# Moving the last 64-row block of a relational basis mix from TensorE to ScalarE and GpSimd, with interleaved one-hots

## The chip, the cores and the metric

One core of one Trainium2 chip. The time is that of one execution of the whole program on the device, in microseconds; less is better. Before the change, three runs took 917.99, 918.70 and 922.83 us, median 918.7 us.

## The reference

A graph of 1250 nodes (512 features) and 21250 edges goes through four graph layers, each followed by a residual sum and a layer norm:

```python
x = _layernorm(x + _L0_gnn_ref(x, edge_index, ...))    # GCN, batch norm, gelu
x = _layernorm(x + _L1_gnn_ref(x, src, dst, ...))      # two SAGE layers
x = _layernorm(x + _L2_gnn_ref(x, edge_index, edge_type_2, ...))   # two relational layers
x = _layernorm(x + _L3_gnn_ref(x, edge_index, ...))    # GIN
```

A relational layer first mixes its weights out of 30 bases of 512 x 512 f32 numbers, for two relations: `w = einsum('rb,bio->rio', att, basis)`. The change is about this mix for the first of the two relational layers.

## The kernel before

The kernel opens with a count stage. It turns the edge list into a dense matrix of edge counts, source node by target node and relation, which all later layers use as a matmul operand. The target nodes are cut into 40 windows of 32 nodes. The edges are sorted by target, in 170 chunks of 128 edges, and a window covers five or more chunks. For each chunk VectorE makes two f16 one-hot matrices in SBUF: `oh_lo` (128 edges x 128, the low 7 bits of the source; stationary operand) and `oh_key` (128 x 640, made of target in the window, relation and source tile; moving operand). TensorE multiplies them (L572, two matmuls of 320 columns a chunk) and sums over the window's chunks in PSUM.

- VectorE, `windows` (L1155): for each window `lows_of` (L1151) makes the four fixed chunks' `oh_lo` in one tensor_tensor (is_equal of an iota and of `lo_h`, whose innermost step is 0); `key_of` (L1140) makes one `oh_key` each; a loop makes `oh_lo` and `oh_key` (L1145, L1140) of the chunks beyond four (one in most windows, two in some). It waits until TensorE has finished the window before the last (`s_win`), so it can be about one window ahead. Once in four windows `sum_counts` (L1178, L1180) adds the two relations of a finished tile. Between windows 9 and 14 it also reduces the input's maximum (L1285, L1288) and a weight's (L1216), and after window 17 computes scales.
- ScalarE, `tile_out`: copies each window's PSUM to SBUF (L766), copies turned tiles out (L772), copies a finished group of the mix (L779) and stores it by DMA (L782), and from window 19 on splits one input tile every second window (L807, L809).
- GpSimd: subtracts to make the low half of each of these ten input tiles (L547, f32 and f16 operands in SBUF).
- TensorE, after each window's product: turns a tile's counts (L597), degrees (L605), and then `mix` (L620): the first relational mix. The stationary operand `mixT` holds attention factors times a folded identity, the moving one a pair of bases' 64 rows (128 partitions x 512 f32). 15 matmuls, one a pair of bases, sum up 64 rows of both relations (partitions 0 to 63 and 64 to 127) in PSUM bank `T[:, 1]`. There are 8 such groups. Group 0 runs ahead of window 0; the other 105 matmuls are handed out by `GROUP_BLOCKS`, two or three after each window.
- SyncE issues the loads in a fixed order: `load_mix` into 8 slots, each when TensorE has freed the slot (`s_mx`).

After window 39 the first unit's dense matmuls begin (L666), for which ScalarE issues DMA transposes (L828) and TensorE turns the last counts (L597). The semaphore `s_mxst` guards the mix results in DRAM (`mixd`), which the fourth unit reads.

Of the kernel before, what the change touches and what calls it, by code (L numbers as in the profile page):

```python
# [8 lines left out]
P = 128  # L9
# [9 lines left out]
FIXED = 2  # L19
# [7 lines left out]
GROUPS = 2 * KT  # L27
MIX_SLOTS = 8
# [20 lines left out]
def resnorm_gnn_kernel(nc, x, src_t, dst_t, typ_t, dst_r, W0, b0, gamma, beta,  # L49
# [11 lines left out]
    with ctx:  # L61
# [86 lines left out]
        dstr = hview(4 * 2 * P).bitcast(i32).rearrange("p (g e) -> p g e", g=2)  # L148
        wlo = hview(4 * NWIN).bitcast(f32)
# [14 lines left out]
        mix_in = [stage[:, q, :] for q in range(KT)] + [zview(4 * D).bitcast(f32) for _ in range(MIX_SLOTS - KT)]  # L164

# [50 lines left out]
        s_xin, s_xmax, s_s0 = sem("s_xin"), sem("s_xmax"), sem("s_s0")  # L216
# [3 lines left out]
        s_gmax = sem("s_gmax")  # L220
# [4 lines left out]
        s_eye, s_mixT = sem("s_eye"), sem("s_mixT")  # L225
        mx_full = [sem(f"mx_full{i}") for i in range(MIX_SLOTS)]
        s_mx = sem("s_mx")
        s_mxe = sem("s_mxe")
        s_mxst = [sem(f"s_mxst{i}") for i in range(2)]
# [36 lines left out]
        b_idf, b_one, b_dg, b_row, b_rev = (sem("b_" + n) for n in ("idf", "one", "dg", "row", "rev"))  # L266
# [24 lines left out]
        GROUP_BLOCKS = [6, 6, 6, 6, 5, 5, 6]  # L291
        assert sum(GROUP_BLOCKS) == NWIN and len(GROUP_BLOCKS) == GROUPS - 1
# [139 lines left out]
        Z_SCALED = 38  # L432
# [17 lines left out]
        def _(sp):  # L450
# [50 lines left out]
        def _(pool):  # L501
# [13 lines left out]
            pool.partition_all_reduce(rngr, rng, P, RMAX).then_inc(s_rngr, 1)  # L515
            pool.memset(epsc[:, :], EPS).then_inc(s_const, 1)
            pool.memset(onec[:, :], 1.0).then_inc(s_const, 1)
            pool.memset(ones, 1.0).then_inc(b_one, 1)
# [22 lines left out]

            pool.wait_ge(s_xin, 1)
            pool.partition_all_reduce(xmax[:, :], xin[:, :], P, RMAX).then_inc(s_xmax, 1)
# [12 lines left out]
            pool.partition_all_reduce(gmax[:, :], gin[:, :], P, RMAX).then_inc(s_gmax, 1)  # L556
# [10 lines left out]
        def _(pe):  # L567

            def chunk_product(slot, j, start=False, stop=False):

                for b in range(2):
                    last = nc.tensor.matmul(Dp[:, j, b, 0:HALF], oh_lo[:, ds(slot * P, P)],  # L572
# [52 lines left out]
            pe.wait_ge(s_const, 10)  # L625
# [11 lines left out]
            assert mixed[0] == PAIRS * GROUPS  # L637
            pe.wait_ge(s_ate, 5 * (NT - 1))
            pe.wait_ge(s_mxe, GROUPS)
# [118 lines left out]
        def _(act):  # L758
# [804 lines left out]
```

## Time and profile before

| | |
|---|---|
| median of three runs | 918.7 us |
| the profiled execution | 917.2 us |
| its span, first to last instruction | 915.4 us |
| TensorE matmul busy | 882.8 us, 96% |
| VectorE busy | 656.2 us, 72% |
| ScalarE busy | 280.8 us, 31% |
| GpSimd busy | 87.9 us, 10% |

The shares are means over the whole program, whose stages have different limits; the count stage is its first 183.66 us.

### The profile page before, as it was taken

Reading aid. Unit: us, or ns where it says so; the run is one execution under the profiler, and the core shown is the slowest. Engines: PE = TensorE matmul, PEld = TensorE weight load, DVE = VectorE, ACT = ScalarE, POOL = GpSimd, SP = SyncE. Lnnn points to the kernel's source line nnn. Section 1 sums busy time; section 2 is a strip of 40 time slices with the busy share of each in tenths; the row PEclk is TensorE's granted clock in tenths of the full one; section 3 lists DMA queues with packets and bytes.
Section 4 is the critical chain, followed back from the end, with each engine's and each line's share of the span. In section 5 each row is a group of like instructions: output and inputs, shape, how many; then the busy total and the mean of one; then the engine's idle time right before and its main releaser. Section 6 shows DMA issues by size and latency. Waiting matters only on the chain.

```text
span 915.4 us, 12673 instructions
## 1 busy us (share of the span) xinstructions
PE 882.8 (96%) x4258; PEld 428.2 (47%) x4258; DVE 656.2 (72%) x1286; ACT 280.8 (31%) x431; POOL 87.9 (10%) x66
## 2 busy tenths in 40 slices
PE   7999999999959999899997999999999999999997
PEld 3555555554545444344443444444444444444443
DVE  6898978658987797998999988975324255552247
ACT  0333444637752116222312111114311221132221
POOL 1000111301220003021210000003200020020000
PEclk9999999999979999999998999999999999999999
DMA  8955665596435885788464655530131014322228
GB/s 275 352 168 165 183 188 191 149 238 198 155 95 157 200 236 150 208 207 204 128 150 108 155 141 161 139 91 1 35 81 23 12 47 139 82 62 41 47 60 237
DMA packets 134888, 129.50 MB, mean 141 GB/s; under 512 B 80687, under 2 KB 81156, under 8 KB 134826
## 3 DMA queue, kind: packets, MB, share of 16 engines
q10 hardware_dynamic: 96192, 60.25, 26.1%
q1 hardware_dynamic: 38634, 68.45, 24.9%
q8 instruction: 36, 0.59, 0.3%
q14 instruction: 26, 0.21, 0.1%
HBM read 97.80 MB, written 12.52 MB: 121 GB/s over the span
## 4 chain that ended last, share of the span: by engine, by line
PE 68%; DVE 15%; DMA 8%; ACT 4%; issue 2%; POOL 1%; DVEq 1%; ACTq 0%; SPq 0%
PE Dp L696 25%; PE Dp L666 24%; PE T L620 11%; PE Dp L572 6%; DVE acc L1262 4%; DMA stage<-in_basis 3%; DMA wst<-mixd 2%; DMA xr<-xres 2%; DVE Zraw L1373 1%; ACT W L1010 1%; DVE stt L1354 1%; ACT wst L863 1%; DVE w L1391 1%; PE T L666 1%; POOL Zraw L530 1%
## 5 line engine op out<-in xcount | busy, mean ns | idle before, releaser
L666 PE MATMUL Dp<-W,hT 128*128 128x512 f16 x792 | 175.7, 381 | 3.6 <-DMA hT<-S 3.6
L696 PE MATMUL Dp<-Zraw,A 128*128 128x512 f16 x800 | 173.0, 379 | 0.0
L1262 DVE SCALAR_TENSOR_TENSOR acc<-stage,att,acc 128x512 f32<-128x512 f32 x232 | 163.5, 770 | 4.3 <-DMA stage<-in_basis 4.3
L696 PE MATMUL Dp<-Zraw,AT 128*128 128x512 f16 x600 | 130.0, 379 | 0.0
L666 PEld LDWEIGHTS Dp<-W,hT 128*128 128x128 f16 x792 | 77.8, 98 | 96.6 <-DMA hT<-S 3.8
L696 PEld LDWEIGHTS Dp<-Zraw,A 128*128 128x128 f16 x800 | 78.2, 98 | 94.4
L696 PEld LDWEIGHTS Dp<-Zraw,AT 128*128 128x128 f16 x600 | 58.7, 98 | 70.8
L1140 DVE TENSOR_SCALAR Zraw<-hT,w 128x640 f16<-128x640 f16 (+1 forms) x209 | 85.9, 456 | 0.3
L1391 DVE SCALAR_TENSOR_TENSOR w<-Dp,aggc,S 128x512 f32<-128x512 f32 x40 | 29.9, 747 | 59.9 <-PE Dp L696 54.0
L962 ACT ACTIVATE Zraw<-Dp,zsc 128x512 f16<-128x512 f32 x46 | 29.4, 684 | 125.8 <-PE Dp L666 121.7
L620 PE MATMUL T<-stage,W 128*128 128x512 f32 x120 | 60.5, 627 | 5.5 <-DMA stage<-in_basis 5.5
L572 PE MATMUL Dp<-Zraw 128*128 128x320 f16 (+1 forms) x418 | 63.7, 299 | 0.4 <-DVE Zraw L1140 0.3
L1331 DVE SCALAR_TENSOR_TENSOR Zraw<-Dp,zsc,Zraw 128x512 f16<-128x512 f32 x26 | 19.5, 749 | 58.6 <-ACT Zraw L962 58.6
L1001 ACT ACTIVATE w<-w,s_in 128x512 f32<-128x512 f32 x30 | 21.6, 720 | 121.0 <-DVE w L1391 116.0
L530 POOL TENSOR_TENSOR W<-wst,W 128x1024 f16<-128x1024 f32 x18 | 42.8, 2395 | 158.6 <-ACT W L866 158.6
L572 PEld LDWEIGHTS Dp<-Zraw 128*128 128x128 f16 (+1 forms) x418 | 40.6, 98 | 36.9 <-issue 23.2
L620 PE MATMUL T<-Zraw,W 128*128 128x512 f32 x120 | 57.4, 601 | 0.0
L666 PE MATMUL Dp<-W,stage 128*128 128x512 f16 x240 | 52.8, 379 | 1.2 <-DVE Zraw L1331 1.2
L766 ACT ACTIVATE Zraw<-Dp 128x640 f16<-128x640 f32 x40 | 28.1, 703 | 78.4 <-PE Dp L572 76.3
L721 PE MATMUL Dp<-AT,Zraw 128*128 128x512 f16 (+1 forms) x240 | 43.4, 344 | 0.0
L1151 DVE TENSOR_TENSOR Zraw<-hT,Zraw 128x512 f16<-128x512 f16 x40 | 28.5, 712 | 20.8 <-PE Dp L572 15.0
L962 ACT ACTIVATE Zraw<-Dp 128x512 f16<-128x512 f32 x26 | 15.5, 596 | 74.6 <-PE Dp L666 72.0
(176 smaller groups left out, 950.4 us busy)
## 6 DMA issues: line engine op xcount, KB each, us to landing
stage<-in_basis SPq DMA_DIRECT2D x180, 256.0 KB, 2.9
Zraw<-in_basis SPq DMA_DIRECT2D x60, 256.0 KB, 3.1
xres<-w ACTq DMA_DIRECT2D x30, 256.0 KB, 2.3
xr<-xres ACTq DMA_DIRECT2D x30, 256.0 KB, 3.1
wst<-in_Wn ACTq DMA_DIRECT2D x4, 1024.0 KB, 5.6
wst<-in_Ws ACTq DMA_DIRECT2D x4, 1024.0 KB, 6.0
wst<-mixd ACTq DMA_DIRECT2D x4, 1024.0 KB, 6.0
wst<-in_root ACTq DMA_DIRECT2D x3, 1024.0 KB, 6.7
```

The lines of the kernel that those rows point to most:

```text
L530: pool.tensor_tensor(weights_of(u, m)[:, 1, 2 * h:2 * h + 2, :], source, weights_of(u, m)[:, 0, 2 * h:2 * h + 2, :], ALU.subtract).then_in ...
L572: last = nc.tensor.matmul(Dp[:, j, b, 0:HALF], oh_lo[:, ds(slot * P, P)], oh_key[:, ds(slot * KEYS + b * HALF, HALF)], start=start, stop=stop)
L620: nc.tensor.matmul(T[:, 1, :], mixT[:, b * P:(b + 1) * P], mix_in[n % MIX_SLOTS], start=(b == 0), stop=(b == PAIRS - 1)).then_inc(s_mx, 1)
L666: last = nc.tensor.matmul(dense_bank(u, t, m), turned[:, hp, k * P:(k + 1) * P], weights_of(u, m)[:, wp, k, :], start=(n == 0), stop=(n == ...
L696: last = nc.tensor.matmul(sum_bank(t), a[:, k, ds(t * P, P)], Z[:, r, h, k, :], start=(n == 0), stop=(n == count - 1))
L721: last = nc.tensor.matmul(Df[:, j, c:c + w], Z[:, 0, h, k, b * P:(b + 1) * P], AT[:, k, c:c + w], start=(k == 0 and h == 0), stop=(k == NT ...
L766: nc.scalar.activation(B[:, t % 2, :, :, a:a + WIN].rearrange("p s r (b d) -> p b (s r) d", b=2), Dp[:, w % 2, 0:2, 0:HALF].rearrange("p b ...
L962: nc.scalar.activation(Z[:, r, 0, ds(t, 1), :], dense_rows(u, t, r), ACT.Copy, scale=scale).then_inc(s_zhi[u], 1)
L1140: return v.tensor_scalar(oh_key[:, ds(slot * KEYS, KEYS)], iota_n, wkey[:, w:w + 1], key_f[:, ds(c, 1)], ALU.add, ALU.is_equal)
L1151: v.tensor_tensor(oh_lo[:, slot * P:(slot + n) * P].rearrange("p (c k) -> p c k", c=n), iota_n[:, 0:P].rearrange("p (c k) -> p c k", c=1). ...
L1262: last = v.scalar_tensor_tensor(part, stage[:, q, :], a, part, ALU.mult, ALU.add)
L1391: v.scalar_tensor_tensor(w1[:, j:j + 1, :], sum_bank(t).rearrange("p (a d) -> p a d", a=1), c, rest, ALU.mult, ALU.add).then_inc(s_pre[u], 1)
```

## The change

- The mix on TensorE has 7 groups instead of 8: 105 matmuls in all instead of 120, 90 of them handed out after windows (`GROUP_BLOCKS` from `[6, 6, 6, 6, 5, 5, 6]` to `[7, 7, 7, 7, 6, 6]`).
- The last 64 rows of both relations are made elsewhere. Per basis, two DMAs of 64 rows each bring the same 64 rows of one basis into partitions 0 to 63 and 64 to 127 of a `bias` buffer (two buffers). After windows 8 to 37 ScalarE scales one basis by its attention column (`late_scaled`), in place, and GpSimd adds it to `late_sum` (29 adds; the first basis is scaled straight into the sum). After window 39 ScalarE stores the sum by two DMAs (`late_out`).
- SyncE's loads are interleaved: `load_late(b)`, which waits until the buffer's add is done (`l_done`), then the next two or three `load_mix`.
- `lows_of` writes the four fixed chunks' `oh_lo` interleaved (chunk innermost), and TensorE reads each as stationary operand with a step of four elements. A new iota, each number repeated four times, stands against `lo_h`, so that no operand has an innermost step of 0.
- Some semaphores are merged, and one initial wait counts the new iota.

```diff
+PE_GROUPS = GROUPS - 1
+LATE_FROM = 8
-        GROUP_BLOCKS = [6, 6, 6, 6, 5, 5, 6]
+        GROUP_BLOCKS = [7, 7, 7, 7, 6, 6]
...
+            for r in range(REL):
+                sp.dma_start(late_att[r * 64:(r + 1) * 64, :], att1[2 + r:3 + r, :].broadcast_to([64, BASES])).then_inc(e_att, 16)
+            def load_late(b):
+                wait(sp, l_done, b - 1)
+                for r in range(REL):
+                    sp.dma_start(late_in[b % 2][r * 64:(r + 1) * 64, :],
+                                 basis1[PE_GROUPS, b // 2, b % 2 * 64:(b % 2 + 1) * 64, :]).then_inc(l_full[b % 2], 16)
+            at = PAIRS + 2 * NT
+            for b in range(BASES):
+                nxt = PAIRS + 2 * NT + (PAIRS * PE_GROUPS - PAIRS - 2 * NT) * (b + 1) // BASES
+                load_late(b)
+                load_mix(at, nxt)
+                at = nxt
+            sp.wait_ge(l_done, BASES)
...
+            def late_add(end):
+                for b in range(late[0], end):
+                    pool.wait_ge(l_sc, b + 1)
+                    if b:
+                        pool.wait_ge(l_done, b)
+                        pool.tensor_tensor(late_sum, late_sum, late_in[b % 2], ALU.add).then_inc(l_done, 1)
+                    else:
+                        pool.sem_inc(l_done, 1)
+                late[0] = end
+            late_add(6)
             pool.wait_ge(s_xin, 1)
...
+            late_add(8)
             reduce_weights(0)
             for t in range(NT):
+                late_add(12 + 2 * t)
                 pool.wait_ge(x_hi, t + 1)
...
+                if isinstance(slot, int):
+                    n = 2 * FIXED
+                    four = slot // n * n
+                    low = oh_lo[:, four * P:(four + n) * P].rearrange("p (k c) -> p k c", c=n)[:, :, slot % n]
+                else:
+                    low = oh_lo[:, ds(slot * P, P)]
...
+            def late_out():
+                act.wait_ge(l_done, BASES)
+                for r in range(REL):
+                    act.dma_start(mixd[r, PE_GROUPS * 64:GROUPS * 64, :],
+                                  late_sum[r * 64:(r + 1) * 64, :]).then_inc(s_mxst[PE_GROUPS % 2], 16)
+            def late_scaled(b):
+                if b == 0:
+                    act.wait_ge(e_att, 64)
+                act.wait_ge(l_full[b % 2], 16 * REL * (b // 2 + 1))
+                nc.scalar.activation(late_in[b % 2] if b else late_sum, late_in[b % 2], ACT.Copy,
+                                     scale=late_att[:, b:b + 1]).then_inc(l_sc, 1)
             def tile_out(t):
                 for i in range(PER):
                     w = PER * t + i
                     window_out(w)
+                    if 0 <= w - LATE_FROM < BASES:
+                        late_scaled(w - LATE_FROM)
...
             for t in range(NT):
                 tile_out(t)
                 weight_work("counts", 0, t)
-            act.wait_ge(s_const, 10)
+            late_out()
+            act.wait_ge(s_const, 11)
...
-                v.tensor_tensor(oh_lo[:, slot * P:(slot + n) * P].rearrange("p (c k) -> p c k", c=n),
-                                iota_n[:, 0:P].rearrange("p (c k) -> p c k", c=1).broadcast_to([P, n, P]),
-                                lo_h[:, ds(c, n)].rearrange("p (c k) -> p c k", k=1).broadcast_to([P, n, P]), ALU.is_equal)
+                v.tensor_tensor(oh_lo[:, slot * P:(slot + n) * P].rearrange("p (k c) -> p k c", c=n),
+                                iota_c.rearrange("p (k c) -> p k c", c=n),
+                                lo_h[:, ds(c, n)].rearrange("p (k c) -> p k c", k=1).broadcast_to([P, P, n]), ALU.is_equal)
```

## Rows read from the trace of the kernel before

**Rows 1.** Busy time by stretch: bounds, length, busy time (count) per engine, clock, DMA.
```profile
21.20:58.75 37.55, 37.55 (x195) 20.99 (x193) 29.95 (x80) 12.14 (x20) 0.00 (x0) 1.00 0.84 285
58.75:133.35 74.60, 74.23 (x425) 41.92 (x424) 65.24 (x165) 31.40 (x53) 6.30 (x7) 1.00 0.59 178
133.35:183.66 50.31, 50.31 (x283) 28.41 (x280) 36.13 (x85) 27.01 (x43) 13.20 (x8) 1.00 0.59 172
```
**Rows 2.** The chain that ended last: start, length, what.
```profile
46.91 1.36 PE Dp L572 x10
...
93.49 1.82 PE T L620 x4
...
129.14 1.36 PE Dp L572 x10
130.50 0.22 PE Dp L597 x4
130.72 2.63 PE T L620 x6
...
183.66 0.91 issue
```
**Rows 3.** Waits of VectorE, 53.8 to 125 us: total, times, longest.
```profile
DVE Zraw L1151 <- PE Dp L572: 0.6, 1, 0.6
```
**Rows 4.** The same, 125 to 176 us.
```profile
DVE Zraw L1151 <- PE Dp L572: 8.9, 6, 2.1
```
**Rows 5.** VectorE and TensorE in order of time: start, length, instruction, idle before it.
```profile
48.49 0.69 DVE L1151 TENSOR_TENSOR Zraw<-hT,Zraw 128x512 f16<-128x512 f16 x1 [1.00 <-PE Dp L572]
...
53.86 0.69 DVE L1151 TENSOR_TENSOR Zraw<-hT,Zraw 128x512 f16<-128x512 f16 x1 [0.62 <-issue]
...
75.02 1.15 DVE L1140 TENSOR_SCALAR Zraw<-hT,w 128x640 f16 x3
...
75.09 1.95 PE L572 MATMUL Dp<-Zraw 128*128 128x320 f16 x10 [0.27 <-DVE Zraw L1140]
...
123.78 1.15 DVE L1140 TENSOR_SCALAR Zraw<-hT,w 128x640 f16 x3
...
174.43 1.33 DVE L1140 TENSOR_SCALAR Zraw<-hT,w 128x640 f16 x3
```
**Rows 6.** Groups by line and shape, 0 to 240 us: busy, mean ns.
```profile
L1151 DVE TENSOR_TENSOR Zraw<-hT,Zraw 128x512 f16<-128x512 f16 x40 | 28.5, 712 | 20.8 <-PE Dp L572 15.0 <-issue 5.7
...
L1178 DVE TENSOR_TENSOR AT<-Zraw 128x1280 f16<-128x1280 f16 x10 | 8.2, 816 | 5.8 <-ACT Zraw L766 5.8
```
**Rows 7.** VectorE's small tensor_tensor and two key pairs, in order of time.
```profile
103.25 0.23 DVE L1180 TENSOR_TENSOR AT<-AT,ident 128x128 f16<-128x128 f16 x1
...
104.70 0.80 DVE L1140 TENSOR_SCALAR Zraw<-hT,w 128x640 f16<-128x640 f16 x2
...
107.31 1.64 DVE L1140 TENSOR_SCALAR Zraw<-hT,w 128x640 f16<-128x640 f16 x2
...
152.02 1.06 DVE L1180 TENSOR_TENSOR AT<-AT,ident 128x128 f16<-128x128 f16 x1
```
**Rows 8.** GpSimd in order of time (three of ten such subtractions).
```profile
107.59 1.16 POOL L547 TENSOR_TENSOR S<-w,S 128x512 f16<-128x512 f32 x1 [6.88 <-ACT S L809]
...
124.63 1.31 POOL L547 TENSOR_TENSOR S<-w,S 128x512 f16<-128x512 f32 x1 [4.74 <-ACT S L809]
...
150.97 2.02 POOL L547 TENSOR_TENSOR S<-w,S 128x512 f16<-128x512 f32 x1 [7.23 <-ACT S L809]
```
**Rows 9.** Weight loads by line and shape, 0 to 240 us: busy, mean ns.
```profile
L572 PEld LDWEIGHTS Dp<-Zraw 128*128 128x128 f16 x320 | 31.0, 98 | 32.9 <-issue 22.8 <-DVE Zraw L1140 0.7 <-ACT Zraw L766 0.5
...
L620 PEld LDWEIGHTS T<-stage,W 128*128 128x128 f32 x120 | 22.1, 199 | 25.3 <-issue 19.3 <-DVE W L1093 5.4 <-DMA stage<-in_basis 0.5
```
**Rows 10.** ScalarE's scaling of a tile, its wait for TensorE, SyncE's wait.
```profile
L807 ACT ACTIVATE w<-acc,s_in 128x512 f32<-128x512 f32 x8 | 5.8, 727 | 2.4 <-issue 2.4
...
ACT Zraw L766 <- PE Dp L572: 75.2, 35, 3.6
...
SPq L458 <- PE T L620: 110.7, 92, 3.3
```
**Rows 11.** Behind the count stage, in order of time.
```profile
184.50 1.13 ACTq L782 DMA_DIRECT2D mixd<-gw  x2
...
191.46 0.23 DVE L1315 CAST gw<-ident 128x128 f32<-128x128 f16 x1
...
192.74 0.61 ACT L772 ACTIVATE A<-Dp 128x512 f16<-128x512 f32 x1
193.04 0.65 PEld L597 LDWEIGHTS Dp<-ident,Zraw 128*128 128x128 f16 x8
```

More of the change, by code:

```diff
@@ L148, in resnorm_gnn_kernel @@
         dstr = hview(4 * 2 * P).bitcast(i32).rearrange("p (g e) -> p g e", g=2)
+        iota_c = dstr.bitcast(f16).rearrange("p g e -> p (g e)")
         wlo = hview(4 * NWIN).bitcast(f32)
@@ L164, in resnorm_gnn_kernel @@
         mix_in = [stage[:, q, :] for q in range(KT)] + [zview(4 * D).bitcast(f32) for _ in range(MIX_SLOTS - KT)]
+        late_att = att[:, 0, :]
+        late_in = [bias[:, i, :] for i in range(2)]
+        late_sum = zview(4 * D).bitcast(f32)
         W2 = W[:, 2, :, :, :].rearrange("p h k d -> p (h k d)")
@@ L228, in resnorm_gnn_kernel @@
         s_mxe = sem("s_mxe")
+        l_full = [sem(f"l_full{i}") for i in range(2)]
+        l_done = sem("l_done")
+        l_sc = sem("l_sc")
         s_mxst = [sem(f"s_mxst{i}") for i in range(2)]
@@ L265, in resnorm_gnn_kernel @@
         s_xst = {u: [sem(f"s_xst{u}_{j}") for j in range(2)] for u in LN}
-        b_idf, b_one, b_dg, b_row, b_rev = (sem("b_" + n) for n in ("idf", "one", "dg", "row", "rev"))
+        b_dg, b_row, b_rev = (sem("b_" + n) for n in ( "dg", "row", "rev"))
         b_ev, b_st, b_mv, b_sd, b_co, b_g = (sem("b_" + n) for n in ("ev", "st", "mv", "sd", "co", "g"))
@@ L289, in resnorm_gnn_kernel @@
         DG = Dp[:, 1, 2, 0:2 * NT]
-        GROUP_BLOCKS = [6, 6, 6, 6, 5, 5, 6]
-        assert sum(GROUP_BLOCKS) == NWIN and len(GROUP_BLOCKS) == GROUPS - 1
+        GROUP_BLOCKS = [7, 7, 7, 7, 6, 6]
+        assert sum(GROUP_BLOCKS) == NWIN and len(GROUP_BLOCKS) == PE_GROUPS - 1
         SHARES = [(i + 1) * PAIRS // n - i * PAIRS // n for n in GROUP_BLOCKS for i in range(n)]
@@ L431, in resnorm_gnn_kernel @@
         XS_FROM = 19
-        Z_SCALED = 38
+        Z_SCALED = 39
         def halves_split(u):
@@ L515, in _ @@
             pool.partition_all_reduce(rngr, rng, P, RMAX).then_inc(s_rngr, 1)
+            pool.iota(iota_c, [[1, P], [0, 2 * FIXED]], base=0, channel_multiplier=0, **kw).then_inc(s_const, 1)
             pool.memset(epsc[:, :], EPS).then_inc(s_const, 1)
             pool.memset(onec[:, :], 1.0).then_inc(s_const, 1)
-            pool.memset(ones, 1.0).then_inc(b_one, 1)
+            pool.memset(ones, 1.0).then_inc(s_const, 1)
             def reduce_weights(u):
@@ L569, in chunk_product @@
             def chunk_product(slot, j, start=False, stop=False):
+                if isinstance(slot, int):
[4 more added lines that the diff above has]
+                    low = oh_lo[:, ds(slot * P, P)]
                 for b in range(2):
-                    last = nc.tensor.matmul(Dp[:, j, b, 0:HALF], oh_lo[:, ds(slot * P, P)],
+                    last = nc.tensor.matmul(Dp[:, j, b, 0:HALF], low,
                                             oh_key[:, ds(slot * KEYS + b * HALF, HALF)], start=start, stop=stop)
@@ L624, in _ @@
             mix(PAIRS)
-            pe.wait_ge(s_const, 10)
+            pe.wait_ge(s_const, 11)
             pe.wait_ge(s_tbl, 1)
@@ L869, in load_bias @@
             def load_bias(u):
+                if u == 1:
+                    act.wait_ge(l_done, BASES)
                 if u > 2:
@@ L1087, in _ @@
             dve.wait_ge(s_const, 8)
-            v.tensor_tensor(eye, ident[:, 0:P // 2], ident[:, P // 2:P], ALU.add).then_inc(s_eye, 1)
-            dve.wait_ge(s_eye, 1)
+            link(v.tensor_tensor(eye, ident[:, 0:P // 2], ident[:, P // 2:P], ALU.add))
             def mix_table(a0, a1):
@@ L1135, in _ @@
             dve.wait_ge(s_tbl, 1)
-            dve.wait_ge(s_const, 8)
+            dve.wait_ge(s_const, 9)
             def key_of(w, slot, c):
```

28 lines of the change are left out of this document (13 added, 15 removed).

## The prediction

> **What bounds the kernel now.** I read the busy time by stretch, the chain of waits, VectorE's waits, and then VectorE and GpSimd in order of time. In the count stage TensorE is busy in all but 0.4 of 162 us [rows 1], and the chain consists of its products (L572) and mix matmuls (L620) with hardly a gap [rows 2]. So TensorE bounds the stage, but VectorE stands close behind. From the one-hots of window 10 (53.86) to the last key of window 27 (123.78 + 1.15 = 124.93) it waited for TensorE 0.6 us in 71.07 [rows 3, 5]. Only from there to 175.76 (174.43 + 1.33) does it have room, 8.9 us in 50.8 [rows 4, 5]. In window 14 TensorE was even held by it: ten products took 1.95 us instead of the 1.36 of the chain [rows 2, 5].
>
> **TensorE's part.** Four L620 records, two matmuls, last 1.82 us in the chain, and six 2.63 [rows 2]; the difference is 0.81 to 0.88 a matmul. I take 0.87. Fifteen fewer are 13.1 us off TensorE. By GROUP_BLOCKS they leave as follows: through window 9, 25 become 21 (3.5 us); windows 10 to 27, 47 become 39 (7.0); windows 28 to 39, 33 become 30 (2.6). What is left of this depends on VectorE.
>
> **VectorE's part, gain.** The 40 four-chunk one-hots take 0.71 us each, a tensor_tensor of 512 elements. The one of 1280 elements whose innermost step is 1 throughout takes 0.82 [rows 6], and that of 128 takes 0.23 [rows 7]. On the line between them 512 elements take 0.43. Undisturbed the old form takes 0.69 [rows 5], so I take 0.26 saved per window, 10 us in all. Bounds: nothing (its rows of four elements may hold it at the old rate) to 0.35; a loss I exclude, since the new form has as many elements and no operand that is read worse than one at a time. The Trainium skill (VectorE: DVE Perf Modes, What auto-detection actually checks) says that 16-bit tensors with step 1 go at two a cycle; by the two measured durations the trace agrees, and by that rule alone the gain would be the same.
>
> **VectorE's part, cost.** This is the step on which I decide. GpSimd's subtraction of 512 elements (1.16 us) began at 107.59, within VectorE's pair of keys, which then took 1.64 us instead of 0.80 [rows 7, 8]. At 150.97 GpSimd's took 2.02, and the small tensor_tensor of VectorE behind it 1.06 instead of 0.23 [rows 7, 8]. The two engines hold each other up: of ten subtractions in the stage seven lengthened VectorE's instruction by 0.83 to 0.89, one by 0.46, and two fell largely into its idle time, as that of 124.63, after which VectorE had nothing to do anyway [rows 8]. The 29 added adds are of the same size and kind, two SBUF inputs. I price one at 0.78 us of VectorE where it is busy. Bounds: 0 (all in gaps or beside reductions) to 1.2. The Trainium skill (SBUF — State Buffer, Who interferes with whom) states a rule that speaks against this change: a two-input instruction of VectorE, or one in a two-port mode, and a GpSimd instruction share a port pair, and the loser is blocked for the whole instruction; reductions are spared. The trace agrees, with 0.84 us. By the rule's full length each add would cost 1.16, and 18 adds 7 us more than I take.
>
> **The sum, stretch by stretch.**
> Up to window 9: VectorE's window 9 waits for the products of window 7 (46.91 + 1.36 = 48.27, start 48.49 [rows 2, 5]). Two mix matmuls are gone ahead of it, 1.74, and one faster one-hot behind it, 0.26. So window 10 starts on VectorE at 53.86 − 2.0 = 51.86.
> Windows 10 to 27: VectorE's work was 71.07 − 0.6 = 70.5. Minus 18 × 0.26 = 4.7, plus 18 adds: two of them fall beside the maximum reductions, so 16 × 0.78 = 12.5. It comes to 78.3, and VectorE ends window 27 at 130.2. TensorE alone would take 7.0 less than 74.6 [rows 1], 67.6, so it is bound by VectorE there. TensorE ended window 14 0.9 us after VectorE's last key (75.09 + 1.95 = 77.04 against 75.02 + 1.15 = 76.17 [rows 5]); so window 27 ends at 131.1, against 130.5 before [rows 2]: +0.6.
> Windows 28 to 39: VectorE had 50.83 − 8.9 = 41.9. Minus 12 × 0.26 = 3.1, plus ten adds, 7.8: 46.6. TensorE needs 183.66 − 130.50 − 2.6 = 50.6 [rows 2]. TensorE bounds: the stage ends at 181.7, 2.0 us earlier than before. (VectorE would end at 176.8, and 0.9 + 0.2 + 2.6 behind it is 180.5.)
>
> **Behind the stage.** late_out puts two more DMA issues into ScalarE's queue, by the two of the row 1.13 us [rows 11]. Behind them stand the table load, the transposes, the first scaled tile and the copies of the last counts. TensorE's last turn (193.04) began right after the copy of 192.74 had its predecessor done, with some 0.2 us to spare [rows 11]; I take +0.7, bounds 0 to 1.1. VectorE's wait for the stores ahead of L1315 (191.46) is covered: they go out by about 186.8.
>
> **At nothing.** 30 scalings of 0.73 on ScalarE: it waited 75.2 us in the stage for TensorE's windows, 35 times [rows 10]; they cost 22, and a copy of a window is needed only a window later. Cover gone, a window would slip by 0.7. GpSimd is idle most of the stage, 19.5 us busy in 162 [rows 1]. SyncE: load_late(b) waits for the add of b − 2, behind which stand mix loads; at that time mixes for 1.3 windows, some 5 us, are loaded, and the queue waited for TensorE 110.7 us [rows 10]. The doubled reads of the last rows (7.9 MB for 3.9) meet DMA engines 0.59 busy [rows 1]. The fifth iota and the merged semaphores lie under the start's loads. The stationary operand with step 4: now a weight load shows 98 ns beside products of 136 (1.36 / 10), the f32 one 199 [rows 2, 9]. I take 0 (hidden up to 136); at 199 it would be 320 × 0.063 = 20 us on TensorE.
>
> Sum: −2.0 + 0.7 = −1.3 us, on 917.2 of the profiled execution (span 915.4 and 1.8 around it): 915.9. The median shown is 1.5 higher, so 917.4.
>
> **Rivals.** 0.5% of this kernel, 4.6 us, is what a measurement can tell from no change.
> (a) The adds cost VectorE little: they start mostly beside reductions, small instructions and gaps, 0 to 0.4 each. For: two of ten did. Against: VectorE has no gaps in windows 10 to 27. At 0.4, that stretch falls by 16 × 0.38 = 6.1, and the whole by 7.4: 911.3. At 0, TensorE's 13.1 less 0.7: 906.3. From 0.57 an add downward it is faster by over 4.6. Chance 0.27.
> (b) The one-hots don't gain (rows of four). Then 4.7 more in windows 10 to 27, and in the last stretch VectorE needs 49.7, still under 50.6: −1.3 + 4.9 = +3.6, 922.3. Chance 0.10, mostly under the bound.
> (c) Slower: the step of four elements lengthens the weight load. Its place is the 320 products of the fixed chunks, its price what it has beyond 136 ns, and it decides against the change from 136 + 13.1 / 320 = 177 ns. At 199 TensorE is at −13.1 + 20.2 + 0.7 = +7.8, with VectorE hidden: 926.5. Against: the f16 load has 38 ns of room. Chance 0.10.
> (d) An add costs VectorE GpSimd's whole 1.16: in windows 10 to 27 16 × 0.38 = 6.1 more, in the last stretch VectorE reaches 50.4 and ties with TensorE: +4.8, 923.5. Chance 0.08. (This is what the page on SBUF named above would make of it.)
> (e) The change doesn't bring the relief it says, because ScalarE holds a window back for a late tile (l_full): 30 waits at 0.3 would be 9 us on ScalarE, hidden by its 75. 0.02; 918.
>
> **Chances.** Forecast 0.43, own range 914.5 to 920.5. Faster: (a)'s 0.25 and 0.03 of the forecast, 0.28. Slower: (c) 0.10, (d) 0.06, (b) and the forecast's edge 0.05, 0.21. Same 0.51. The range takes in half prices of (a) and the full 1.16 of (d): 907.5 to 924.
>
> **What the profile will show.** L620 with 15 fewer matmuls; VectorE's L1151 at 0.4 us undisturbed; GpSimd with 29 adds of 1.2 us or more, each beside a VectorE instruction lengthened by 0.8; VectorE without waits for TensorE in windows 10 to 27, and TensorE instead waiting for L1140 or L1151 by some 7 us there; L572 weight loads at or near 98 ns, products at 136; first dense product at about 182.6 instead of 184.57. Wrong if TensorE keeps its gapless chain (then (a)), or if the products' pace grows (then (c)).

## The result, and the profile after

The changed kernel takes 935.4 us (median of 4 runs, 931.27 to 938.23) against 919.2 for the kernel before (917.99 to 922.83); the ratio is 1.0186, 95% interval 1.0162 to 1.0209. The forecast was 917.4 us, no change that can be measured, with a range up to 924. The kernel is slower by some 17 us, over twice the 7.8 us of the slowest rival. Below, a difference of 1% stands for 9.2 us.

| | before | after |
|---|---|---|
| span of the profiled execution | 915.4 | 929.5 |
| count stage ends, on TensorE | 183.66 | 197.30 |
| from there to the end | 731.7 | 732.2 |
| TensorE busy from 21.20 to the stage's end | 162.1 of 162.5 | 158.7 of 176.1 |

All of it lies in the count stage. The busy times by stretch, for the changed kernel, with the columns of [rows 1]:

```profile
21.20:58.75 37.55, 36.53 (x195) 21.52 (x196) 31.94 (x91) 12.92 (x22) 1.27 (x1) 1.00 0.84 283
58.75:133.35 74.60, 63.34 (x351) 36.74 (x348) 61.91 (x139) 34.61 (x58) 27.37 (x20) 0.93 0.63 181
133.35:197.30 63.95, 58.85 (x325) 33.87 (x324) 59.03 (x111) 40.70 (x66) 31.27 (x22) 0.97 0.64 191
```

TensorE, busy in all but 0.4 us before, is idle 11 us in the second stretch and 5 in the third; its granted clock is 0.93 and 0.97 there, where it was 1.00. Finer rows show where: 0.87 from 85 to 98 us, in which TensorE is busy 7.3 of 13 us, and 0.76 in the 14 us behind them. VectorE is idle too in the second (61.9 of 74.6), so it does not simply bound. GpSimd's row has 27.4 us busy of 74.6, which still looks like an engine with time to spare. Read in order of time it is not (start, length, instruction, idle before it):

```profile
9.41 0.59 POOL L541 PARTITION_ALL_REDUCE w<-w  x1 [6.43 <-issue]
17.81 1.19 POOL L542 IOTA hT<- 128x512 f16 x1 [7.81 <-issue]
...
71.11 1.26 POOL L578 TENSOR_TENSOR Zraw<-Zraw,bias 128x512 f32<-128x512 f32 x1 [2.04 <-ACT bias L847]
78.32 0.51 POOL L585 PARTITION_ALL_REDUCE xmax<-xin  x1 [5.95 <-issue]
85.84 2.67 POOL L578 TENSOR_TENSOR Zraw<-Zraw,bias 128x512 f32<-128x512 f32 x2 [7.01 <-issue]
95.56 0.38 POOL L549 PARTITION_ALL_REDUCE mwg<-mw  x1 [7.05 <-issue]
102.59 2.79 POOL L578 TENSOR_TENSOR Zraw<-Zraw,bias 128x512 f32<-128x512 f32 x2 [6.65 <-issue]
```

Each time GpSimd goes here from an iota or an add to a partition_all_reduce, or back, 5.95 to 7.81 us pass with no instruction and no one that it waits for ("issue"). The kernel before had such gaps as well, at the start and far behind the stage. Its one change inside the windows, from the reduction of 72.02 to the subtraction of 99.55, had 26.68 us of waiting for ScalarE to hide in. Its order of time shows these two, which I had not weighed:

```profile
9.77 0.65 POOL L515 PARTITION_ALL_REDUCE w<-w  x1 [6.79 <-issue]
...
266.85 0.37 POOL L556 PARTITION_ALL_REDUCE gmax<-gin  x1 [5.94 <-issue]
```

The chain of the changed kernel goes through the third gap of the stage, and its end shows who ends the stage now (start, length, what):

```profile
88.74 6.82 issue
95.56 0.39 POOL mwg L549
...
188.58 2.04 DVE Zraw L1214
190.62 2.23 DVE Zraw L1209
...
197.30 0.91 issue
```

Where TensorE's mix matmuls stood [rows 2] stand a reduction that comes late and VectorE's one-hots (L1209, L1214), far over their own 0.44 us and 0.25 us. From 96 to 193 us the chain holds 1.2 us of TensorE; nearly all the rest is VectorE and its queue. What VectorE meets at the end is not only the late adds. Behind its last instruction of the stage GpSimd makes the low half of a weight (`low_weights`, two subtractions of 1024 columns, some 2.1 us each). In the kernel before they began behind VectorE's last key (174.43 + 1.33 = 175.76); in the changed kernel they began at 188.36, inside VectorE's last window, and one low (2.12 us instead of 0.25) and the keys behind it (3.02 instead of 1.15) took 3.7 us longer. GpSimd before, GpSimd after, VectorE after:

```profile
176.91 4.21 POOL L530 TENSOR_TENSOR W<-wst,W 128x1024 f16<-128x1024 f32 x2
...
188.36 4.30 POOL L557 TENSOR_TENSOR W<-wst,W 128x1024 f16<-128x1024 f32 x2
...
188.50 2.12 DVE L1214 TENSOR_SCALAR Zraw<-hT,w 128x128 f16 x1
190.54 3.02 DVE L1209 TENSOR_SCALAR Zraw<-hT,w 128x640 f16 x3
```

The waits of the changed kernel from 40 to 200 us (total, times, longest) name the same two, and a third:

```profile
ACT bias L847 <- DMA bias<-in_basis: 23.5, 13, 4.8
DVE tmpc L1265 <- POOL mwg L549: 9.4, 1, 9.4
PE Dp L622 <- DVE Zraw L1209: 9.4, 5, 4.7
```

VectorE stood 9.4 us for the weight maximum; up to window 17 it had lost 0.4 us (its one-hots start at 83.43, at 83.02 before), and window 18 starts at 98.76 instead of 89.23. ScalarE, which also copies the windows out, waited 23.5 us for late half-tiles.

### The profile page after: what moved, and what is told of

Read it like the earlier page. It is cut to its first block, busy times and chain, and to the rows that moved or that the text cites. A ratio compares the mean times of both kernels' runs of the same rounds, so it can differ in the third digit from the quotient of the medians.

```text
span 929.5 us, 12756 instructions
## 1 busy us (share of the span) xinstructions
PE 877.6 (94%) x4228; PEld 427.6 (46%) x4228; DVE 673.1 (72%) x1286; ACT 299.0 (32%) x460; POOL 129.4 (14%) x96
## 4 chain that ended last, share of the span: by engine, by line
PE 52%; DVE 20%; issue 5%; DMA 5%; ACT 4%; DVEq 3%; POOL 1%; ACTq 0%; POOLq 0%
PE Dp L716 25%; PE Dp L746 24%; DVE acc L1331 4%; DVE Zraw L1209 3%; DVE stt L1422 1%; DVE Zraw L1441 1%; ACT W L1080 1%; DMA wst<-mixd 1%; DVE w L1459 1%; DMA stage<-in_basis 1%; ACT wst L930 1%; PE T L716 1%; DMA xr<-xres 1%; POOL Zraw L557 1%; DVEq L1233 1%
## 5 line engine op out<-in xcount | busy, mean ns | idle before, releaser
L1209 DVE TENSOR_SCALAR Zraw<-hT,w 128x640 f16<-128x640 f16 (+1 forms) x209 | 100.7, 527 | 0.5 <-issue 0.4
L622 PE MATMUL Dp<-Zraw 128*128 128x320 f16 (+1 forms) x418 | 67.1, 304 | 11.3 <-DVE Zraw L1209 10.7
L622 PEld LDWEIGHTS Dp<-Zraw 128*128 128x128 f16 (+1 forms) x418 | 45.1, 111 | 48.4 <-issue 34.4
L670 PE MATMUL T<-stage,W 128*128 128x512 f32 x106 | 56.1, 653 | 5.4 <-DMA stage<-in_basis 5.4
L578 POOL TENSOR_TENSOR Zraw<-Zraw,bias 128x512 f32<-128x512 f32 x29 | 40.5, 1397 | 89.6 <-ACT bias L847 75.6
L670 PE MATMUL T<-Zraw,W 128*128 128x512 f32 x104 | 52.4, 622 | 0.1
L549 POOL PARTITION_ALL_REDUCE mwg<-mw x7 | 2.6, 378 | 348.0 <-DVE mw L1275 340.9
```

Source lines behind the costliest of these rows:

```text
L578: pool.tensor_tensor(late_sum, late_sum, late_in[b % 2], ALU.add).then_inc(l_done, 1)
L622: last = nc.tensor.matmul(Dp[:, j, b, 0:HALF], low, oh_key[:, ds(slot * KEYS + b * HALF, HALF)], start=start, stop=stop)
L670: nc.tensor.matmul(T[:, 1, :], mixT[:, b * P:(b + 1) * P], mix_in[n % MIX_SLOTS], start=(b == 0), stop=(b == PAIRS - 1)).then_inc(s_mx, 1)
L1209: return v.tensor_scalar(oh_key[:, ds(slot * KEYS, KEYS)], iota_n, wkey[:, w:w + 1], key_f[:, ds(c, 1)], ALU.add, ALU.is_equal)
```

## The experiments

Theory at the start: GpSimd's gaps between reductions and other operations (G), on top of the forecast's port cost. Rivals: the adds alone, at a higher price than 0.78 us (A); the new one-hots or their weight loads (O); the ring of load, scale and add that holds ScalarE (R). The kernels of this section are compared with the kernel before on the same chip.

### 1 to 4: the gaps and the adds

1, the weight maximum moved next to that of x:

```diff
-            late_add(8)
             reduce_weights(0)
+            late_add(8)
```

> The two partition reductions on GpSimd in the middle of the count stage (of the input's and of a weight's maximum) stand directly behind one another, instead of with adds 6 and 7 between them. Theory S (GpSimd pays some 6 to 7 us each time it goes from tensor_tensor to the reduction or back: gaps of 5.95, 7.01, 7.05 and 6.65 us in the changed kernel's trace): two gaps of four go, VectorE's wait of 9.4 us for the weight's maximum goes, and the stage ends 5 to 8 us earlier: 928 to 931 us against 935.4. Theory P (the adds hold VectorE up at the port and nothing else matters): the same adds, no change, 935. Theory L (the late tile's ring of load, scale, add with two buffers holds ScalarE): little change, 934 to 936, since add 6 comes no earlier.

Measured: 928.7 us, ratio 1.0137 (1.0102 to 1.0172). One of the two pairs of gaps is gone, and 0.5% with it (the two intervals overlap at the edge).

2, both reductions inside the stage as plain copies, all adds kept:

```diff
-            pool.partition_all_reduce(xmax[:, :], xin[:, :], P, RMAX).then_inc(s_most, 1)
+            pool.tensor_copy(xmax[:, :], xin[:, :]).then_inc(s_most, 1)
...
-            reduce_weights(0)
+            pool.tensor_copy(mwg[:, 0:1], mw[:, 0:1]).then_inc(s_mwr, 1)
```

> Both reductions in the middle of the count stage are replaced by a copy of each partition's own maximum, so the scales are no longer those of the whole tensor (the output is not the reference's). All adds stay. Theory S: no gap of 6 to 7 us is left in GpSimd's row between 60 and 110 us; the 8.7 us lost between windows 17 and 18 come back and one or two more: 924 to 927 us. Theory P: unchanged, 935. Theory L: unchanged or 1 us less.

Measured: 926.1 us, 1.0093 (1.0071 to 1.0115). In its order of time on GpSimd the copy stands right behind an add, with no gap:

```profile
71.38 1.27 POOL L578 TENSOR_TENSOR Zraw<-Zraw,bias 128x512 f32<-128x512 f32 x1 [2.03 <-ACT bias L848]
72.58 0.79 POOL L585 COPY xmax<-xin 128x1 f32<-128x1 f32 x1
```

So the gap belongs to the change of operation and costs this kernel about half of its loss (1.0186 to 1.0093). The adds alone are not the whole cause; A falls as the only one.

3, iota_c in a buffer of its own, filled ahead of the first reduction:

```diff
+            pool.iota(iota_c, [[1, P], [0, 2 * FIXED]], base=0, channel_multiplier=0, **kw).then_inc(s_const, 1)
             pool.wait_ge(s_rng, 1)
             pool.partition_all_reduce(rngr, rng, P, RMAX).then_inc(s_rngr, 1)
-            pool.iota(iota_c, [[1, P], [0, 2 * FIXED]], base=0, channel_multiplier=0, **kw).then_inc(s_const, 1)
```

> The repeated iota has a buffer of its own and is made ahead of the first partition reduction on GpSimd, not behind it. Theory S: the gap of 7.81 us in front of it goes, VectorE makes the first one-hots at about 15.2 us as in the kernel before and not at 20.2, window 10 begins on VectorE some 2 us earlier; the later stalls stay: 932 to 934 us. Rival (the lead of 5 us is eaten by windows 10 to 14, where VectorE bounds, or by the wait for the reductions): 935, no change.

Measured: 935.4 us, 1.0216 (1.0189 to 1.0244), no gain: a miss. VectorE's first one-hots do start at 15.26 again, and window 10's at 52.17, where the forecast had 51.86. But the number of changes stays the same: the one that lay between reduction and iota lies now between reduction and the first add. That add begins 3.6 us after its half-tile is scaled (54.06 + 0.71 = 54.77 on ScalarE), where the changed kernel's begins 0.1 us after. GpSimd in order of time, in this run:

```profile
10.39 0.63 POOL L542 PARTITION_ALL_REDUCE w<-w  x1 [6.25 <-issue]
...
58.33 3.32 POOL L578 TENSOR_TENSOR Zraw<-Zraw,bias 128x512 f32<-128x512 f32 x2 [47.09 <-issue]
79.61 0.44 POOL L585 PARTITION_ALL_REDUCE xmax<-xin  x1 [7.48 <-issue]
```

The two reductions come 1.3 us later than in the changed kernel, and VectorE waits 11.0 us for the second instead of 9.4. What was won at the start was lost there.

4, no add at all (the semaphore is counted up in its place):

> GpSimd's 29 adds are left out (it only hands the semaphore on; one term of the mix remains, so the output is not the reference's). Loads, scalings and stores stay. Both S and P: TensorE bounds the stage again, 15 mix matmuls less: 908 to 912 us, some 2 us of it lost at the start through the late iota. Theory L (the loads and the scalings cost by themselves): 918 or more.

Measured: 911.9 us, 0.9942 (0.9924 to 0.996). The forecast's sum for adds at no price was 906.3 us, 0.9865. So something besides gaps and adds is missing too (this kernel keeps the start's gap ahead of the iota).

### 5 to 8: the one-hots

5, the kernel before with nothing but the interleaved one-hots (iota ahead of the reduction):

> The kernel before with only the interleaved one-hots (repeated iota in a buffer of its own, ahead of the first reduction). My forecast's step: the one-hots take 0.43 us, VectorE's windows follow each other 0.26 us sooner, TensorE still bounds: within 1 us of before, with VectorE waiting some 8 us more for TensorE. Theory Q (found in the trace of the run without adds: windows on VectorE start 2.60 us apart with one-hots of 0.43 or 0.69 alike, since its sequencer's register work sets the pace): same time, and back-to-back windows still 2.60 us apart. If the weight load with a step of four costs TensorE (rival c of the prediction), the products' pace of 136 ns grows and the time with it.

Measured: 916.9 us, 0.9984 (0.9975 to 0.9994), the only kernel that computes everything and is faster than the one before, by 1.5 us. Its groups by line and shape, 0 to 250 us (busy, mean ns, idle before):

```profile
L580 PE MATMUL Dp<-Zraw 128*128 128x320 f16 x320 | 56.5, 299 | 0.0
L580 PEld LDWEIGHTS Dp<-Zraw 128*128 128x128 f16 x320 | 36.2, 113 | 28.4 <-issue 21.7 <-ACT Zraw L774 0.5 <-DVE Zraw L1148 0.3
L1159 DVE TENSOR_TENSOR Zraw<-iota_cT,Zraw 128x512 f16<-128x512 f16 x40 | 20.1, 502 | 24.6 <-PE Dp L580 18.0 <-issue 6.3
```

The weight load with step four is 113 ns instead of 98 [rows 9] and hidden; the products stay at 299 ns, as before. That settles rival (c) of the prediction. The one-hots take 502 ns instead of 712 [rows 6], 8.4 us less in all. Of these 1.5 us come out; VectorE waits for TensorE 18.0 us instead of 15.0, and from 14 to 184 us it stands 13.1 us instead of 9.6 for nothing that the profile names ("issue").

6, 7 and 8 are the changed kernel, number 4 and number 2 with the one-hots as they were and no fifth iota:

> The changed kernel with the old form of the one-hots (and without the repeated iota and its switch on GpSimd). Forecast's step (0.26 us a window gained on VectorE): undoing it costs 4 to 7 us, less 1 to 2 for the start: 938 to 940. Theory Q: it costs nothing and the start gives 0 to 2: 933 to 935.

> As the run without adds (one term of the mix remains), and with the old one-hots. Forecast's step: 2 to 4 us slower than that run's 0.994 of before. Theory Q: the same or 1 to 2 us faster, 0.992 to 0.994 of before.

> The changed kernel with the old one-hots and both middle reductions as copies of each partition's own maximum (output not the reference's): the only long gap of GpSimd left is that in front of the first reduction. Forecast's price of the adds (0.78 us of VectorE each) with no gain from the one-hots gave 922.3 for before at 918.7, that is 1.004 of before. Theory Q together with a dearer chain of adds: 1.006 to 1.010, as the run with copies alone (1.009).

Measured: 939.5 us, 1.0251 (1.0214 to 1.0287); 910.9, 0.9928 (0.9911 to 0.9944); 929.6, 1.012 (1.0103 to 1.0137). Without adds the new one-hots bring nothing (0.9942 against 0.9928, within the intervals). With all adds and gaps they bring 0.65% (1.0251 to 1.0186), with adds and copies 0.3% (1.012 to 1.0093, intervals that overlap): they help where VectorE is held up. Why not otherwise shows in VectorE's order of time, the kernel before first and the changed one below it, windows 16 and 17:

```profile
80.42 0.69 DVE L1151 TENSOR_TENSOR Zraw<-hT,Zraw 128x512 f16<-128x512 f16 x1 [0.20 <-issue]
...
83.02 0.69 DVE L1151 TENSOR_TENSOR Zraw<-hT,Zraw 128x512 f16<-128x512 f16 x1
```

```profile
80.83 0.56 DVE L1220 TENSOR_TENSOR Zraw<-hT,Zraw 128x512 f16<-128x512 f16 x1 [0.21 <-issue]
...
83.43 0.56 DVE L1220 TENSOR_TENSOR Zraw<-hT,Zraw 128x512 f16<-128x512 f16 x1
```

Two windows follow each other by 2.60 us both times, though nothing is waited for and the one-hots are 0.13 shorter. In the chain of the changed kernel VectorE's queue (DVEq: L449, L1233, L1214) has pieces of its own between the instructions of a window. Where a late add has held VectorE up just before, the queue is ahead, and the distance does shrink: 2.28 us from 106.42 to 108.70 in the changed kernel, with one-hots of 0.41. So O has no loss in it; the gain is covered in undisturbed windows and comes out in disturbed ones.

### 9 to 12: what is left without the gaps

9, iota ahead and the two copies. One change of operation is left in the stage, between the first reduction and the first add; the prediction counted none.

> The changed kernel with the fifth iota ahead of GpSimd's first reduction (a buffer of its own) and with the two reductions inside the stage (the largest entry of x, the first weight maximum) replaced by plain copies: a scale comes out different, no value is the reference's. GpSimd then changes nowhere between a reduction and adds on the stage's path, which is what the prediction assumed. If the prediction's other terms are right (adds 0.78 us each, one-hots 0.26 us saved, TensorE 13.1 us relieved), this is its 917 us, ratio 0.996 to 1.003. If the one-hots' saving and part of TensorE's relief are not there either (windows on VectorE stay 2.60 us apart, as in the runs so far), it stays near the copies alone, 1.004 to 1.009.

Measured: 923.9 us, 1.0069 (1.0044 to 1.0094). Against the changed kernel the gaps cost 1.17%, 10.7 us. The change that is left makes the first add begin 3.9 us after its half-tile is scaled (57.93 against 53.34 + 0.71), and ScalarE waits 1.8 us for the fourth half-tile; number 13 has the same, and the changed kernel has not. It is not the forecast's 917: some 7 us have another cause.

10, number 8 with a third buffer for the late half-tiles:

> The copies in place of the two reductions, the old one-hots and no fifth iota (as in the eighth run, ratio 1.012), and a third buffer for the late half-tiles; the reductions' values are missing. If the ring of two buffers (load, scale, add, next load) held ScalarE and with it the windows, this run is 3 us or more faster than the eighth, 1.009 or less. If the adds cost by holding VectorE off, the third buffer changes nothing: 1.010 to 1.014, and VectorE's busy time per one-hot stays.

Measured: 930.5 us, 1.0127 (1.008 to 1.0173), the same as number 8. ScalarE's wait for late loads is 5.6 us, against 4.2 in number 8. The interval reaches down to 1.008, so a small gain isn't excluded, but R falls as the main cause for this spacing. It isn't nothing: the chain of number 9, with two buffers, goes once through a late half-tile, 3.43 us at 131.16.

11, number 1 and number 3 together, nothing left out:

> The changed kernel, nothing left out, with the fifth iota ahead of the first reduction and the reduction of the first weight maximum moved next to that of x's maximum. If the start's gap and the middle's gaps are separate costs, this is paired alone (1.0137) less up to 4 us, 1.009 or so. If VectorE is caught up by TensorE either way (as with the iota alone), it is 1.011 to 1.015.

Measured: 925.9 us, 1.009 (1.006 to 1.0119), as expected, though number 3 alone had gained nothing; the intervals of numbers 1 and 11 overlap. It is the best kernel with the adds in it that computes everything, and still slower than the one before.

12, the late work moved behind window 18, three items in two windows, iota ahead:

> The changed kernel, nothing left out: iota ahead, and the late half-tiles scaled and added three in two windows from window 19 on, behind both of the stage's reductions; GpSimd then changes once from reductions to adds in the stage, with nobody waiting for it, and no add falls into windows 0 to 18. TensorE's mixing shares before window 19 are as in the kernel before, its relief lies behind. If the cost is place (the gaps, and adds where VectorE bounds), window 18 is reached as before (89 us on VectorE) and the rest pays 29 adds x 0.95 = 27 us on VectorE against its idle 15 us and 13 us of relief on TensorE: a ratio of 0.997 to 1.005. If an add costs the stage the same wherever it lies (14 us for 29), it is 1.008 to 1.015.

Measured: 942.7 us, 1.0246 (1.0197 to 1.0295), a miss of both expectations. Its order of time on GpSimd, ScalarE and TensorE shows the cause (three views of one stretch, put together by time):

```profile
96.75 0.71 ACT L847 ACTIVATE bias<-bias,att 128x512 f32<-128x512 f32 x1
...
104.03 1.26 POOL L579 TENSOR_TENSOR Zraw<-Zraw,bias 128x512 f32<-128x512 f32 x1 [32.63 <-issue]
...
109.16 0.72 ACT L847 ACTIVATE bias<-bias,att 128x512 f32<-128x512 f32 x1 [6.22 <-DMA bias<-in_basis]
...
113.11 0.61 PE L647 MATMUL Dp<-ident,Zraw 128*128 128x128 f16 x4 [7.33 <-ACT A L822]
```

The scaled half-tile is there at 97.46; the add begins 6.6 us later, since the change comes in front of it (GpSimd's last operation was the reduction of 70.55). The next load needs the buffer that this add frees, ScalarE waits 6.22 us for the load, and TensorE 7.33 for a copy that stands behind it in ScalarE's queue. I had said "with nobody waiting for it". The same gap again, in a third place.

### 13 to 16: the parts of the remaining 7 us

13 is number 9 with adds of 8 columns:

```diff
-  pool.tensor_tensor(late_sum, late_sum, late_in[b % 2], ALU.add).then_inc(l_done, 1)
+  pool.tensor_tensor(late_sum[:, 0:8], late_sum[:, 0:8], late_in[b % 2][:, 0:8], ALU.add).then_inc(l_done, 1)
```

> As the ninth run (iota ahead, copies for the two reductions, 1.0069), but each of the 29 adds covers 8 columns in place of 512; every wait and GpSimd instruction is kept, most of the late sum is missing. If an add costs by the time that it holds VectorE off, its price goes with its length: 0.993 to 0.997, as without adds. If it costs as a link of the ring or by the order of waits on GpSimd, it stays above 1.002.

Measured: 913.9 us, 0.996 (0.9944 to 0.9976). The length of the adds is worth 1.09%, 10.0 us; between this and number 14 lie 0.37%, for the adds' presence whatever their length and the change of operation ahead of the first. VectorE's groups from 56 to 193 us, number 9 first, then number 13 (busy, mean ns):

```profile
L1210 DVE TENSOR_SCALAR Zraw<-hT,w 128x640 f16<-128x640 f16 (+1 forms) x153 | 85.6, 604 | 0.1
L1215 DVE TENSOR_SCALAR Zraw<-hT,w 128x128 f16 x37 | 16.3, 442 | 1.4 <-issue 1.3
L1221 DVE TENSOR_TENSOR Zraw<-iota_cT,Zraw 128x512 f16<-128x512 f16 x28 | 15.1, 541 | 3.9 <-issue 2.1 <-PE Dp L623 1.9
```

```profile
L1210 DVE TENSOR_SCALAR Zraw<-hT,w 128x640 f16<-128x640 f16 (+1 forms) x153 | 65.3, 470 | 1.3 <-issue 1.1
L1221 DVE TENSOR_TENSOR Zraw<-iota_cT,Zraw 128x512 f16<-128x512 f16 x29 | 13.7, 473 | 9.7 <-issue 4.8 <-PE Dp L623 4.7
L1215 DVE TENSOR_SCALAR Zraw<-hT,w 128x128 f16 x37 | 9.9, 267 | 3.2 <-issue 3.1
```

The same keys take 20.3 us more beside long adds, the single lows 6.4, the four-chunk one-hots 28 × 0.068 = 1.9: 28.6 us in all. Not all of it is the adds' own. In number 9 the two subtractions for the weight meet VectorE's last window, as in the changed kernel; in number 13 they begin at 169.53, behind it. GpSimd and VectorE in number 9, then GpSimd in number 13:

```profile
180.23 4.37 POOL L557 TENSOR_TENSOR W<-wst,W 128x1024 f16<-128x1024 f32 x2
...
182.54 2.11 DVE L1215 TENSOR_SCALAR Zraw<-hT,w 128x128 f16 x1
...
169.53 4.22 POOL L557 TENSOR_TENSOR W<-wst,W 128x1024 f16<-128x1024 f32 x2
```

Two lengthenings of some 1.9 us, 3.7 in all, are theirs (an estimate from these rows). That leaves some 25 us for 29 adds, 0.86 each, close to the 0.83 to 0.89 of the kernel before. TensorE waits 0.81 and 1.91 us for the keys of this last window, up to 2.7 of the 10.0 us by which the kernel grows; the rest of VectorE's 28.6 falls into time that it had. The Trainium skill (SBUF — State Buffer, Who interferes with whom) says that the loser is blocked for the whole of the other's instruction; the mean add lasts 1.39 us here and costs some 0.86, so the trace agrees in kind and stays under the full length.

14, no adds, iota ahead; 15, no late loads and scalings beyond the first either; 16, as 15 with the old one-hots:

> The adds left out (a count in their place, the late sum is missing) and the iota ahead of GpSimd's first reduction, both of the stage's reductions as they are. If the start's 5 us were hidden behind TensorE in the run without adds (0.9942), this is the same, 0.993 to 0.996. If they were not, up to 4 us less, 0.990 or so. The forecast's own sum for adds at no price is 906.3 us, 0.9865.

> As the fourteenth, and the 29 late loads and scalings after the first left out too: the last 64 rows of the first basis are not mixed at all, nothing is put in the place of TensorE's 15 matmuls; one-hots interleaved. If the late loads and scalings on ScalarE and the queues kept the relief away, this comes to the forecast's 0.9865 or below (0.985 to 0.989). If VectorE's pace of 2.60 us a window does, it stays within 2 us of the run without adds, 0.991 to 0.995.

> The kernel before with TensorE's 15 matmuls of the last 64 rows simply left out (those rows are not mixed): no late loads, scalings or adds beyond the first, the old one-hots, no fifth iota. The forecast counts 6.1 us for this alone (2.6 behind window 27, 3.5 ahead of window 10, the rest held by VectorE), 0.993. If TensorE's relief shows in full it is 0.986; if VectorE holds nearly all of it, 0.995 to 0.998.

Measured: 910.4 us, 0.9923 (0.9907 to 0.994); 906.3, 0.9891 (0.9867 to 0.9914); 909.7, 0.9911 (0.9894 to 0.9927). The late loads and scalings cost 0.32%, 2.9 us (the two intervals just overlap), though ScalarE waits 37.6 us for TensorE from 40 to 200 us: in number 14 it stands 6.5 us for late half-tiles, and its copies behind them. TensorE's 15 matmuls off, alone, are worth 0.89%, 8.2 us of 13.1; with the new one-hots 10.0 (these two intervals overlap). In number 15 TensorE's products still stand 2.8 us, 2.3 of them for VectorE's keys (group by line, 56 to 176 us):

```profile
L621 PE MATMUL Dp<-Zraw 128*128 128x320 f16 (+1 forms) x308 | 48.0, 299 | 2.8 <-DVE Zraw L1210 2.3
```

### 17 and 18: the place of the adds, once more

Number 12 with one add of a single column right behind the two reductions, so that the change is paid early; number 18 with adds of 8 columns besides.

> The twelfth run (adds from window 19, 1.0246, nothing left out) with one add of a single column behind the two reductions, so that GpSimd's 7 us change is paid in an idle stretch and not ahead of the first late add. If that change cost the twelfth run its 7.3 us on TensorE, this is 1.014 to 1.018. If it is anything else that held window 22, it stays at 1.022 or above. If adds behind window 19 were cheap for lying where VectorE has room, it is under 1.003.

> As the seventeenth, with adds of 8 columns in place of 512 (most of the late sum is missing). The difference of the two is what the adds' length costs from window 19 on; spread over windows 8 to 37 it was 1.0 % (1.0069 to 0.996). What remains over 0.9923 is what three loads and scalings in two windows cost, one behind the other in a ring of two buffers: nothing, if the ring was only slow through the adds; 1 % or more, if the loads themselves can't keep up.

Measured: 937.0 us, 1.0205 (1.0174 to 1.0235), and 923.2, 1.0056 (1.0039 to 1.0073). In number 17, in order of time on GpSimd, the change lies where nobody waits, and the first late add has none before it:

```profile
78.94 0.18 POOL L587 TENSOR_TENSOR xin<-xin 128x1 f32<-128x1 f32 x1 [6.98 <-issue]
98.08 1.42 POOL L579 TENSOR_TENSOR Zraw<-Zraw,bias 128x512 f32<-128x512 f32 x1 [18.96 <-ACT bias L848]
```

TensorE's wait of 7.33 is gone, but its waits for ScalarE's copies still come to 16.6 us (20.8 in number 12), the longest 5.6. Only 0.4% came back, less than I had expected, and the intervals overlap. The length of the adds costs 1.49% here, more than the 1.09% of the spread ones: packed into 20 windows they keep VectorE busy 80.8 of the 95 us from 100 to 195. And the short ones stay 1.3% above number 14: packed, the loads and scalings themselves hold ScalarE (18.8 us of waiting for late half-tiles). So adds behind window 18 are not cheap in this form; a spacing of one per window there would need fewer than 29, and was not tried.

## Why the prediction was wrong

The account, in per cent of the kernel before and in us, from the pairs of runs (each difference is known to some ±2 to 3 us, as its intervals show):

| term | forecast | measured | from |
|---|---|---|---|
| 15 matmuls off TensorE, shorter one-hots | −12.4 | −10.0 (0.9891) | 15 |
| late loads and scalings | 0 | +2.9 | 15 to 14 |
| 29 adds on GpSimd, with what they push aside | +11.1 | +13.4 | 14 to 9 |
| GpSimd's changes of operation (all but one) | 0 | +10.7 | 9 to the changed kernel |
| sum | −1.3 | +17.0 (measured whole: 17.1) | |

**The step that failed** is the one "At nothing": "GpSimd is idle most of the stage", and "The fifth iota and the merged semaphores lie under the start's loads". Both took an engine's free time for time in which it can do anything. GpSimd had 143 us free, but adds put between its two reductions make it pay 6 to 7 us four times, with VectorE (9.4 us) and ScalarE behind it, and the iota came 7.8 us after the reduction instead of under the loads: VectorE started at 20.23 instead of 15.19. That is 10.7 of the 18.3 us missed. The forecast even placed two adds beside "the maximum reductions", as if these could run one behind the other. The row that tells of it, 6.79 and 5.94 us of "issue" ahead of a reduction, is in the trace of before; no rival held it. Both rivals on the slow side, (c) and (d), named other mechanisms.

**TensorE's part** was right in its mechanism and somewhat too high in worth: with adds at no price the forecast had 12.4 us, and 10.0 came with the new one-hots, 8.2 with the old; in number 15 TensorE still stands 2.3 us for VectorE's keys. **The one-hots** were read rightly as to their own length (0.41 at 106.42 and 108.70 in the changed kernel, where 0.43 was forecast, and 0.56 in other places), wrongly as to worth: 0.26 per window was taken off VectorE's time as if its instructions were all that it does. Measured without adds, they give 0.16% (number 5), 0.2% (16 to 15) and −0.14% (7 to 4), of which only the first is clear of noise. Rival (b) had the sign of that, not the reason.

**VectorE's cost**, the step on which I had decided, was mis-sized, not wrong: some 0.86 us of VectorE per add instead of 0.78, between the forecast and rival (d), and 13.4 us of the kernel instead of 11.1. The sum left out that a VectorE that ends later runs into what GpSimd does next: up to 2.7 us on TensorE in number 9 come from the weight's two subtractions and a tile's subtraction that meet the last window. The changed kernel shows it as the rows of before did, key pairs and triples of 1.75 and 2.11 us instead of 0.80 and 1.15 (VectorE in order of time):

```profile
106.42 0.41 DVE L1220 TENSOR_TENSOR Zraw<-hT,Zraw 128x512 f16<-128x512 f16 x1
...
108.70 0.41 DVE L1220 TENSOR_TENSOR Zraw<-hT,Zraw 128x512 f16<-128x512 f16 x1
109.03 1.75 DVE L1209 TENSOR_SCALAR Zraw<-hT,w 128x640 f16<-128x640 f16 x2
...
110.87 2.11 DVE L1209 TENSOR_SCALAR Zraw<-hT,w 128x640 f16 x3
```

**Windows 28 to 39** were forecast as TensorE's. They became VectorE's: the chain ends there in keys and a low lengthened by the weight's two subtractions. The forecast let VectorE end at 176.8, with the first of them at 176.91 in the kernel before. **ScalarE's 30 scalings** at nothing measured 2.9 us: ScalarE works in its program's order, so its waits for half-tiles (6.5 us in number 14) hold the window's copy behind them. **Behind the stage** +0.7 was forecast; the time from the stage's end to the last instruction grew by 0.5. The weight load (98 to 113 ns, hidden) was right.

TensorE's clock adds little to the chain here, though it shows. From 98 to 112 us, granted at 0.76, ten products took 2.83 us instead of the 1.52 of 86.69 (TensorE in order of time):

```profile
86.69 1.52 PE L622 MATMUL Dp<-Zraw 128*128 128x320 f16 x10
...
100.18 2.83 PE L622 MATMUL Dp<-Zraw 128*128 128x320 f16 x10 [4.69 <-DVE Zraw L1209]
```

But the chain goes through VectorE at that time, so these products lie beside it. Not settled is how the 10.7 us divide between VectorE's wait and ScalarE's; no run held the one fixed while the other moved.

## What to carry to other kernels

An engine with idle time is not free for any operation: look in its order of time for idle time put down to "issue" ahead of an operation, and count how many such changes the new order makes and who waits behind each. Price work on GpSimd by the VectorE instructions beside it (here 0.83 to 0.89 us for each GpSimd instruction of 512 columns), first ask whether VectorE has that much room, and then look at what GpSimd does next, which a VectorE that ends later runs into. A shorter instruction on an engine helps only where its instructions, and not its queue, set the distance from one round to the next; two rounds without a wait show which, in undisturbed and in disturbed places.

## What the runs showed of the hardware

GpSimd's change between partition_all_reduce and iota or tensor_tensor costs 5.77 us (changed kernel, reduction at 280.31) to 8.18 (number 2, iota at 18.26), in both directions and wherever no longer wait covers it. memset and a plain copy did not bring it: in number 14 a memset began at 11.36 right behind the reduction of 10.81, and in number 2 a copy stood behind an add without a gap. The Trainium skill (GPSIMD Engine Reference, 2.1 Instruction dispatch) tells of some 6 us, invisible in the profile, at the first call of a freshly loaded kernel; the size agrees, but here it came back at every change. In number 14 GpSimd in order of time:

```profile
10.81 0.68 POOL L542 PARTITION_ALL_REDUCE w<-w  x1 [6.67 <-issue]
11.36 0.18 POOL L543 MEMSET epsc<- 128x1 f32 x1
```

The interleaved one-hot of 512 elements took 0.41 to 0.43 us in some windows and 0.56 in others; what decides between them (I suspect where the window's run of four chunks starts) was not tried. A weight load with a step of four columns took 113 ns instead of 98. In the kernel before, eight of GpSimd's ten subtractions of 512 columns lengthened the VectorE instruction beside them (seven by 0.83 to 0.89 us, one by 0.46); in the changed kernel those of 1024 columns lengthened a low and a group of keys by 1.87 each.
